# Local attention: where TensorE turns the queries, before or behind the next chunk's scores

## What is computed

```python
h = shift_token(x)                       # half of the channels come from the token before
q, k, v = split(h @ wqkv)                # 8 heads of 64
q = l2norm(q) * qs;  k = l2norm(k) * ksc
q, k = rotary_xpos(q, k)
# windows of 64 tokens; each query sees its own window and the one before
sim  = einsum(q * 8, k);  sim = where(mask, -max, sim)
attn = softmax(sim);  o = attn @ v
x = x + o @ wo
```

## Time and profile before

| | us |
|---|---|
| median of 3 runs (2103.34 to 2105.58) | 2104.4 |
| the profiled execution | 2106.7 |
| its span, first to last instruction | 2104.9 |
| PE busy | 1719.8 (82%) |
| DVE busy | 1545.4 (73%) |
| ACT busy | 1215.5 (58%) |
| POOL busy | 931.1 (44%) |

### The profile page before, as it was taken

One profiled execution on the slowest core, in us unless ns is written; L12 is line 12 of the kernel. 1 busy time (PEld: TensorE's weight loads), 2 busy tenths in 40 slices (PEclk: granted clock), 3 DMA queues, 4 the chain that ended last, 5 costly groups with the idle time before them and its releaser, 6 DMA issues. The chain is left out here.

```text
span 2104.9 us, 38118 instructions
## 1 busy us (share of the span) xinstructions
PE 1719.8 (82%) x13216; PEld 959.9 (46%) x13216; DVE 1545.4 (73%) x3211; ACT 1215.5 (58%) x2673; POOL 931.1 (44%) x771
## 2 busy tenths in 40 slices
PE   5889888874899999885991575799998989999884
PEld 2333333332344444442440442566665656666553
DVE  5999999997477777751216475788885778888675
ACT  5778777762244444432444333788885368888621
POOL 5778777783002222222443133555552145555310
PEclk7999999998699999986996787999999999999897
DMA  4433343320311111101514423010000000000010
GB/s 147 123 111 107 115 125 107 106 65 16 106 26 39 41 37 42 42 20 45 147 56 130 140 84 116 11 26 18 17 17 18 19 11 22 22 17 17 19 41 23
DMA packets 107405, 125.56 MB, mean 60 GB/s; under 512 B 28804, under 2 KB 79151, under 8 KB 106224
## 3 DMA queue, kind: packets, MB, share of 16 engines
q1 hardware_dynamic: 103120, 115.07, 19.3%
q0 software_dynamic: 4096, 8.06, 1.2%
HBM read 71.60 MB, written 38.11 MB: 52 GB/s over the span
## 5 line engine op out<-in xcount | busy, mean ns | idle before, releaser
L394 POOL TENSOR_TENSOR m_bu<-m_dtu,m_brow 128x1024 f32<-128x1024 f32 x128 | 299.6, 2356 | 54.6 <-DVE m_hs L818 54.1
L818 DVE TENSOR_TENSOR_SCAN m_hs<-m_ps_da,m_bu 128x1024 f32<-128x1024 f32 x128 | 291.9, 2280 | 6.0 <-POOL m_bu L394 5.5
L1363 ACT ACTIVATE a_pt<-a_ps_s 128x1024 f32<-128x1024 f32 x128 | 131.0, 1024 | 225.6 <-PE a_ps_s L1141 225.6
L523 PE MATMUL m_ps_y_ps<-m_prod,m_ident 128*128 128x512 f32 x512 | 243.4, 598 | 0.0
L2913 ACT ACTIVATE l_pe<-l_ps_s,l_nbias,l_qs 128x128 f32<-128x128 f32 x512 | 226.4, 467 | 15.7 <-DVE l_nbias L3063 15.7
L1480 DVE TENSOR_REDUCE a_mpad<-a_ps_s 128x4 f32<-128x1024 f32 x128 | 156.8, 1225 | 91.6 <-PE a_ps_s L1133 90.5
L1133 PE MATMUL a_ps_s<-a_heads 32*128 32x256 f32 x1024 | 186.7, 444 | 43.5 <-DVE a_mpad L1480 29.0
L670 ACT ACTIVATE m_ps_da<-m_dt,m_a_neg 128x510 f32<-128x510 f32 x256 | 166.0, 681 | 73.1 <-DVE m_hs L818 72.4
L1141 PE MATMUL a_ps_s<-a_qm,a_heads 32*128 32x256 f32 x1024 | 184.3, 437 | 1.6 <-ACT a_pt L1363 1.2
L1067 POOL TENSOR_TENSOR a_rstd<-a_ve,a_mhalf 128x2 f32<-128x2 f32 x48 | 33.8, 705 | 301.5 <-DVE a_ve L1438 162.5
L828 DVE TENSOR_TENSOR m_prod<-m_hs,m_ps_c_ps 128x1024 f32<-128x1024 f32 x128 | 153.2, 1197 | 12.3 <-PE m_ps_c_ps L509 12.3
(11 more groups left out here) (344 smaller groups left out, 4210.6 us busy)
## 6 DMA issues: line engine op xcount, KB each, us to landing
m_brow<-state_rows SPq DMA_DIRECT2D x64, 512.0 KB, 4.3
slots<-m_void SPq DMA_DIRECT2D x16, 516.0 KB, 5.4
l_near<-l_v SPq DMA_DIRECT2D x64, 128.0 KB, 2.3
e_xs<-slots SPq DMA_DIRECT2D x16, 258.0 KB, 2.8
ys<-m_void SPq DMA_DIRECT2D x8, 512.0 KB, 5.4
qk<-a_qk SPq DMA_DIRECT2D x16, 256.0 KB, 2.0
a_heads<-qk SPq DMA_DIRECT2D x64, 64.0 KB
ew_w<-in_w SPq DMA_DIRECT2D x2, 2048.0 KB, 11.9
```

Source lines behind the costliest of these rows:

```text
L394: nc.gpsimd.tensor_tensor(bu[s % 4][:, :, :], dtu[p][:, :, :], b2, ALU.mult).then_inc(bu_rd, 1)
L523: last = pe.matmul(y_ps[:, h, :], ident[:, :], prod[d % 3][:, h, :], start=False, stop=(s == NS - 1))
L818: dve.tensor_tensor_scan(hs[s % 4][:, :, :].rearrange("p h t -> p (h t)"), da[s % 2][:, :, :, :].rearrange("p h q t -> p (h q t)"), bu[s % ...
L1363: nc.scalar.activation(pt[t % 2][:, :, :], s2[:, :, :], ACT.Exp).then_inc(exp_rd, 1)
```

## The change

The queries' turning no longer ends a step. It stands directly behind `scores`: behind those of chunk i the queries of chunk i + 1 are turned, in front of `transpose_r` and `transpose_p`. Each turning thus changes places with the scores that followed it. The first two turnings of a layer (chunks 0 and 1) keep their places. Besides, `turn_q` waits for the square only where it writes into the bank that the square reads. No other engine's program changes.

```diff
                 def turn_q(n, b, c):
                     l, i = at[n], NCH * b + c
                     pe.wait_ge(l.sum_rd[Q], i + 1)
-                    pe.wait_ge(l.sq_rd[Q], i + 1)
+                    if i < kept[Q]:
+                        pe.wait_ge(l.sq_rd[Q], i + 1)
                     at_least(pe, l.xT_sb[Q], i)
                     at_least(pe, l.pT_sb, NU * (i - 2))
...
                         scores(n, b, c)
                         before = (b, 0) if c == 1 else (b - 1, 1)
                         behind = not first or c == 1
+                        if c == 1 and last < 2:
+                            turn_q(n, b + 1, 0)
+                        elif c == 0 and not first:
+                            turn_q(n, b, 1)
                         if c == 1 and last < 1:
                             pe.wait_ge(l.v_sb, NCH * (b + 1) + 1)
                             transpose_r(n, b + 2)
...
                             project_v(n, b + 1, c)
                         if behind:
                             weigh(n, before[0], NU * before[1] + 1)
-                        if last < 2:
-                            turn_q(n, b + 1, c)
```

## The result

The changed kernel takes 2084.3 us (median of 4 runs, 2080.6 to 2086.8), the kernel before 2104.0 (4 runs); the ratio on record is 0.9897, 95% interval 0.9884 to 0.9910; the quotient of the two medians, 0.9906, lies inside it. So it is faster by 19.7 us by the medians and by 21.7 (18.9 to 24.4) by the ratio, where 22.5 were forecast. The profiled execution has a span of 2082.9 us, against 2104.9.

What follows compares the result with a forecast made beforehand. A circle over PE and ACT was taken to set the chunks' pace, with PE having least slack. 30 pairs x 0.72 = 21.6 us plus 1.0 at layer starts gave 22.5 off 2104.4: 2082 us, range 2071 to 2096.

Steps and rivals of the forecast that it cites:

- The idle is the square's: PE's idle before the queries' turning, 0.37 us in c=1, is a wait for ACT's square of the queries.
- The scores follow the weighing after 0.60 us: Last weighing's start to next scores' start: 0.60 and 0.62 us remain of 1.50 and 1.49.
- c=1: E at S + 3.96, then 4.15, then 0.60, in all 8.71: A block's second chunk: scores' start (S) to first exponential (E), to last weighing, to next scores; 8.71 us, was 8.95.
- ACT's copy still ends last: In c=1, ACT's copy of weights, not PE's own 8.51 us, still sets the last weighing.
- c=0: 7.74 + 0.62 = 8.36 by PE: A block's other chunk: scores to last weighing, then to next scores, set by PE; 8.36 us, was 8.84.
- About the middle: In c=0, scores to last weighing taken as 7.74 us, between 7.68 and 7.81, for a hidden wait for ACT's copy.
- A pair 17.07: A c=1 and a c=0 chunk together take 17.07 us instead of 17.79, 0.72 less, 30 times.
- The layers' starts, 0.5 us each: At each layer's start the first freed scores gain 0.96 instead of 0.48 us, about 0.5 more, twice.
- The last block, -0.05: In a layer's last block, scores with an added turning and nothing taken away behind them lose 0.05 us.
- DVE as cover: DVE waits 0.43 us more for the residual, hidden by 0.20 us in c=1; about 0.04 short in c=0.
- The second: Rival: c=1 gains nothing because ACT's copy of queries comes later than reckoned; 2087 to 2096 us, chance 0.15.
- The third: Rival, slower: with x from weighing to scores, a pair takes 15.85 + 2x us; 2108 us and more, chance 0.09.

Runs made afterwards that it cites:

- e5: Kernel before, wait and turning untouched, but on ScalarE the square of the queries stands in front of the copy of the keys; ratio 0.9894.
- e1: Kernel before with the wait for the square dropped and the turning left at the end of the step; ratio 0.9866.
- e7: Changed kernel with the four transposes of the weights' second half issued twice in the c=1 chunks only; ratio 0.9927 to the kernel before.
- e6: Changed kernel with the four transposes of the weights' second half issued twice in the c=0 chunks only; ratio 0.9962 to the kernel before.
- e2: Changed kernel with the wait for the square put back in every turning; ratio 0.9898 to the kernel before.
- e3: Changed kernel, but in c=1 chunks the residual's transposes and ScalarE's shift come before the queries' turning and copy; ratio 0.9883 to the kernel before.
- e8: The changed kernel run again unaltered, as measure for the runs beside it; ratio 0.9895 to the kernel before.
- e9: Repeat of e3's program (residual and shift before the queries' turning and copy) beside the changed kernel; ratio 0.9856 to the kernel before.
- e10: The changed kernel run once more unaltered, in the third sitting; ratio 0.9895 to the kernel before.
- e4: Changed kernel with the square of the queries in front of the copy of the keys on ScalarE; ratio 0.9974 to the kernel before.
- e11: e9 with TensorE's waits in each layer's last block filled by 12 and 24 identity transposes; ratio 0.9850 to the kernel before.

## Why the prediction was right, and where its terms were off

- **The idle is the square's.** Right, by e5 without touching PE's code, and by e1.
- **The scores follow the weighing after 0.60 us.** Measured 1444.91 - 1444.32 = 0.59. The row at the layer's end was the right one to read it from.
- **c=1: E at S + 3.96, then 4.15, then 0.60, in all 8.71.** Measured 1440.15 - 1436.14 = 4.01, 1444.32 - 1440.15 = 4.17, 0.59, in all 8.77. The copy started at S + 2.26 instead of 2.22, and each handover lost a few hundredths. "ACT's copy still ends last" held: 0.21 us idle in front of the weighing, and only 0.16 of 0.44 paid in e7.
- **c=0: 7.74 + 0.62 = 8.36 by PE.** Measured 7.76 and 0.62, so 8.38; e6 shows that PE sets it. "About the middle" for the hidden wait was a choice between two bounds and came out right.
- **A pair 17.07.** It was 17.14 to 17.15. Over 30 pairs this is 2 us: 30 x 0.72 should have been 30 x 0.65. The last blocks' clock, below, hid this error.
- **The layers' starts, 0.5 us each.** The first exponentials of the first five chunks span 33.4 us instead of 35.1, that is 1.7; two pairs give 1.3. So 0.4 each.
- **The last block, -0.05.** Wrong, for a cause that wasn't in the sum. The step to the last chunk's exponentials took 9.23 and 9.72 us before and 7.96 in both layers after. The mask matmuls and scores in it, 1.02 and 1.99 us (the mask row is in the earlier trace rows), were at the lower clock level before, behind a wait of 2.28 us; with the turning inside that block the wait is 1.69 us, and they mostly stay at the upper level. The scores before:

```profile
1599.06 1.99 PE L2678 MATMUL l_ps_s<-l_kT,l_qT 64*64 64x128 f32 x32
```

Over the traces of the old order (before, e1, e5) the step took 9.03 us or more in 6 layers of 6; over those of the new one (after, e2, e3, e8, e9, e10) 7.95 to 7.97 in 10 of 12, and 9.06 and 9.33 in two. e4 and e7 have the new order and the same wait besides their own edits, and there it is 9.50 us or more in three layers of four. So the move has a gain of its own after all, 1.3 to 1.8 us a layer here, and not in every execution. That the shorter wait is the reason is argued from these counts; no run changed it alone. PE of the changed kernel there:

```profile
1589.02 0.34 PE L2724 MATMUL l_ps_o<-l_pT,l_near 128*64 128x64 f32 x4 [1.69 <-ACT l_pT L2925]
...
1590.17 1.10 PE L2679 MATMUL l_ps_s<-l_kT,l_qT 64*64 64x128 f32 x32
```

- **DVE as cover.** Right in kind: from its maxima to the residual it is 4.26 us instead of 3.83, and these are the 0.43 that were reckoned. Only 0.24 of them stand as idle in front of the residual, 0.13 lie further up, where the rotation of the queries starts later behind the sums of squares (0.73 instead of 0.60 us). And the c=1 maxima start with no idle at all, at S + 1.71. In c=0 its slack was forecast as 0.04 short. It shows nowhere, as said, because ACT comes later still.
- **The sum and the clock.** In the profiled pair the two layers' attention gained 24.2 us (first exponential of a layer to the last chunk's first one: 551.7 us to 527.5). Of that 19.5 are the 30 pairs' 0.65, 3.0 the last blocks' clock, 0.9 the starts; the rest, 0.8, lies in the last steps before, where first the shift and then the projections fall away. Forecast for the same stretch were 22.5, so it gained 1.7 more than was reckoned. The first layer's first exponential came 2.1 us later than before (1327.0 and 1329.1 us after the start), which nothing in the change explains; e8, the same program, has it at 1329.3, e6 at 1327.3. That is the scatter of the earlier stages, and why a time of the whole can't test a term of 2 us. The path over the two engines was forecast rightly; that the number for the whole came so near (2084.3 for 2082) is in part luck, since 2 us too many for the pairs, 3 us for the clock that weren't in the sum, and this scatter partly cancel.
- **The rivals.** The second (c=1 gains nothing) was right in its mechanism and small in size: c=1 gained 0.18 of the 0.24. The third's sum was tested by e4: it holds with an x for each kind of chunk (15.93 + 1.01 + 0.71 = 17.65, measured 17.64), and one x for both overstated c=0, where PE hides 0.3 us more. What the prediction missed is not in its number: it reckoned both parts as one gain and didn't ask what the dropped wait alone would bring, which is 17.02 us a pair, where the whole change gives 17.14.

## What to carry to other kernels

When an engine idles in front of a step, look how far behind another engine's row it starts: if that distance stays while the idle changes, it is that row's place in its queue, and an earlier place, a later question or no question all cure it. Of these choose the one that puts nothing in front of the longest stretch of the other queue: here the turning behind the scores cost 0.71 us in front of eight exponentials (3.30 to 4.01), and 0.22 of it came back by letting the shift go first. And reckon the bound for each kind of chunk apart; 0.44 us more of the same work cost 0.43 in one and 0.16 in the other.

## What the runs showed of the hardware that wasn't expected

- Transposes of an identity that nobody needs can take the place of a wait, and the rows behind them ran at TensorE's upper clock level. Twenty-four of them in 2.84 us filled a wait of 3.2 us, and the rows behind were 0.7 to 0.9 us shorter each, in both layers of the one trace (e11); without them 14 layers of 15 with that wait were slowed.
- A wait of 2.28 us was followed by the lower level in all six layers that had it, one of 1.69 us in five of sixteen, and one of 1.24 us (e6) in neither of two. e2 had 9.06 and 7.96 us for the same step in the two layers of one execution, so this can differ where program and wait are the same.
- A matmul's record can be missing at the same spot through a whole trace: 62 of 13216 after the change, the first of the two mask matmuls in every chunk but the second of each layer. So it is in nine of the thirteen traces (after, e1 to e8) and in none of the other four, e10 of the same program among them. Behind a weighing it looks like 0.16 us of idle with no releaser. The count of a group against its weight loads tells it from a wait.
